# A recommendation tower (CIN and dense layers): three instead of four GpSimd adds per block, a sum of 14 instead of ten parts

## The reference

```python
e = jnp.stack([tbl_0[ids[:, 0]], ..., tbl_38[ids[:, 38]]], axis=1)      # (512, 39, 16)
def _cin_layer(X0, Xi, W, b):
    Wr = W.reshape(H, F0_, Fi)
    return jnp.einsum('hjk,bjd,bkd->bhd', Wr, X0, Xi) + b[None, :, None]
for W, b in Ws:                       # three layers, X0 = e throughout
    Xi = _cin_layer(X0, Xi, W, b)
    res.append(Xi.sum(axis=2))        # (512, 128) each
h = jnp.concatenate([z, dense_ctx], axis=1)          # z: the three, (512, 384)
h = jnp.maximum(h @ W_top1 + b_top1, 0.0)
h = jnp.maximum(h @ W_top2 + b_top2, 0.0)
y = h @ W_top3
```

## Time and profile before

| | us |
|---|---|
| median of 3 runs | 710.0 (707.98 to 715.27) |
| profiled execution | 709.59 |
| its span, first to last instruction | 707.8 |
| TensorE busy | 650.3 (92%) |
| VectorE busy | 506.6 (72%) |
| GpSimd busy | 490.1 (69%) |
| ScalarE busy | 479.0 (68%) |

### The profile page before, as it was taken

The page is one execution under the profiler, slowest core; times in us unless marked ns, Lnnn a source line. Parts: engine busy times, 40 slices in busy tenths (PEclk is TensorE's granted clock), DMA queues, the critical chain, the costliest instruction groups (busy, mean ns, idle before and its releaser), DMA issues.

```text
span 707.8 us, 12139 instructions
## 1 busy us (share of the span) xinstructions
PE 650.3 (92%) x2622; PEld 469.6 (66%) x2622; DVE 506.6 (72%) x1177; ACT 479.0 (68%) x1730; POOL 490.1 (69%) x465
## 2 busy tenths in 40 slices
PE   0097889999999999999999999999989999999998
PEld 0055567777677777777787677777767777778763
DVE  2345588979697979798853797979777979784810
ACT  2145577878687878686935778787767868784802
POOL 5767478878787878888854787878786845453700
PEclk9999999999999999999999999999999999999999
DMA  8660425151515151515140041322323040002000
GB/s 208 126 131 12 110 38 114 40 109 27 120 29 118 28 119 28 120 28 118 29 109 13 10 113 17 81 49 67 63 61 67 7 116 4 2 4 81 0 1 0
DMA packets 65776, 44.51 MB, mean 63 GB/s; under 512 B 49563, under 2 KB 58062, under 8 KB 63860
## 3 DMA queue, kind: packets, MB, share of 16 engines
q1 hardware_dynamic: 54610, 39.35, 25.1%
q0 software_dynamic: 5120, 1.29, 2.1%
q10 hardware_dynamic: 6002, 3.39, 1.8%
HBM read 40.78 MB, written 1.94 MB: 60 GB/s over the span
## 4 chain that ended last, share of the span: by engine, by line
PE 71%; DVE 8%; DMA 6%; issue 4%; POOL 4%; SPq 3%; ACT 3%; DVEq 0%; ACTq 0%; POOLq 0%
PE a_ps L525 28%; PE d_ps L525 18%; PE quad_ps L495 11%; DVE x2t L436 6%; PE quad_ps L568 5%; PE g_ps L555 5%; POOL emb L214 3%; ACT parts L697 2%; DMA rows<-x_rows 2%; DVE parts L424 2%; DMA x_rows<-emb 2%; DMA emb<-tables_dram,rows_now 1%; SPq L320 1%; PE a_ps L654 1%; POOL parts L227 1%
## 5 line engine op out<-in xcount | busy, mean ns | idle before, releaser
L697 ACT ACTIVATE parts<-a_ps,xt 128x128 f32<-128x128 f32 x1536 | 426.5, 397 | 117.9 <-PE a_ps L525 113.6
L227 POOL TENSOR_TENSOR parts<-parts 128x512 f32<-128x512 f32 x256 | 327.3, 1294 | 143.8 <-ACT parts L697 141.4
L424 DVE SCALAR_TENSOR_TENSOR parts<-d_ps,xt,parts 128x128 f32<-128x128 f32 x832 | 236.0, 343 | 90.0 <-PE d_ps L525 82.4
L525 PE MATMUL a_ps<-w_hi,x_hi 128*128 128x512 f32 x384 | 178.0, 464 | 1.8 <-ACT x_hi L668 0.9
L214 POOL DMA_INDIRECT emb<-tables_dram,rows_now x160 | 154.0, 962 | 29.1 <-issue 20.6
L436 DVE TENSOR_REDUCE x2t<-parts 128x128 f32<-128x1280 f32 x64 | 157.4, 2459 | 4.2 <-POOL parts L227 4.2
L525 PE MATMUL a_ps<-w_hi,x_lo 128*128 128x512 f32 x384 | 153.6, 400 | 2.9 <-DVE z L405 2.5
L525 PE MATMUL a_ps<-w_lo,x_hi 128*128 128x512 f32 x384 | 152.3, 397 | 1.2 <-ACT xt L678 1.2
L495 PE MATMUL quad_ps<-products,w_sb 117*128 117x512 f32 (+1 forms) x224 | 116.6, 606 | 13.0 <-DVE products L395 13.0
L525 PE MATMUL d_ps<-w_hi,x_hi 128*128 128x512 f32 (+1 forms) x256 | 124.3, 486 | 0.0
L525 PE MATMUL d_ps<-w_lo,x_hi 128*128 128x512 f32 (+1 forms) x256 | 97.6, 381 | 2.5 <-DMA diag<-xt 2.5
(11 more groups left out here) (52 smaller groups left out, 278.1 us busy)
## 6 DMA issues: line engine op xcount, KB each, us to landing
shifted<-x_rows SPq DMA_DIRECT2D x48, 312.0 KB
shifted<-x_rows SPq DMA_DIRECT2D x48, 234.0 KB
diag<-xt SPq DMA_DIRECT2D x256, 4.9 KB
rows<-x_rows SPq DMA_DIRECT2D x48, 78.0 KB
emb<-tables_dram,rows_now POOLq DMA_INDIRECT x160, 2.4
g_sb<-w_dram ACTq DMA_DIRECT2D x3, 832.0 KB, 10.4
w_sb<-w_dram SPq DMA_DIRECT2D x7, 320.0 KB, 3.0
x_rows<-emb SPq DMA_DIRECT2D x32, 40.0 KB
```

What stands on the lines that cost most here:

```text
L227: nc.gpsimd.tensor_tensor(parts[:, i % 2, now:now + GF, :], parts[:, i % 2, now:now + GF, :], parts[:, i % 2, more:more + GF, :], ALU.add) ...
L424: nc.vector.scalar_tensor_tensor(now, d_ps[d % D_RING][:, H * at:H * (at + 1)], xt[:, u, i, j:j + 1], before, ALU.mult, ALU.add).then_inc( ...
L525: return nc.tensor.matmul(bank[:, 0:H * len(fields)], x[:, u, 128 * i:128 * (i + 1)], w[:, fields[0]:fields[-1] + 1, :].rearrange("p j h - ...
L697: last = nc.scalar.activation(parts[:, i % 2, 2 + GF * a + at, :], a_ps[(NA * i + a) % A_RING][:, H * at:H * (at + 1)], ACT.Copy, scale=xt ...
```

## The change

One more of ScalarE's groups is kept as it is: `KEEP` becomes 3 and `PARTS_LEFT` 2 + 3 x 4 = 14. GpSimd adds groups three, four and five onto groups zero, one and two, so no add builds on an earlier one, and the wait at L225 falls away. An add has to wait for the staging of one group more than the add with the same index did. Since there are only three adds in a block, the ten gathers get new places in the same order. Their number, the other engines' programs and all tiles stay.

```diff
@@ -48,7 +48,7 @@
 D_RING, A_RING = 2, 3
 
 
-ADDS = 4
+ADDS = 3
 KEEP = NA - ADDS
 PARTS_LEFT = 2 + KEEP * GF
 
@@ -79,7 +79,7 @@
 FIRST_TILES = 4
 
 ROWS_AT, FIRST_ROWS_AT, SECOND_ROWS_AT = {(1, 4): 2}, {(1, 0): 1, (3, 4): 2}, {(2, 2): 2}
-GATHER_AT = {(0, 1): 0, (0, 3): 1, (1, 1): 2, (1, 2): 3, (1, 3): 4, (2, 1): 5, (2, 3): 6, (3, 1): 7, (3, 2): 8, (3, 3): 9}
+GATHER_AT = {(0, 1): 0, (0, 2): 1, (1, 0): 2, (1, 1): 3, (1, 2): 4, (2, 0): 5, (2, 1): 6, (2, 2): 7, (3, 1): 8, (3, 2): 9}
 
 W2_STEP = FIELDS // HALF_CHUNKS + 1
 W2_FIRST = FIELDS - W2_STEP * (HALF_CHUNKS - 1)
```

## The result

The changed kernel takes 743.67 us in the median of four runs (740.66 to 747.12) against 710.75 us; the ratio is 1.045 (95% interval 1.040 to 1.050). Its profiled execution took 742.4 us, with a span of 740.6. The forecast was 739, between 722 and 746.

The account below looks back on a forecast made before the run. It took TensorE to bound the kernel, held up by VectorE's sum in VectorE's own queue. Terms 30.4 + 2.2 - 0.3 - 2.8 = +29.5 us on 709.6 gave 739.1, stated as 739, range 722 to 746.

Parts of the forecast that it names:

- item 1: Third-block sums of chunks 1 to 14, chunk 14's fourth, three in chunk 15: 18 delays of 0.95 us reach TensorE.
- item 2: Fourth-block sums without slack, chunks 0 to 13 except 11: 13 times, each passing on 0.95 us.
- item 3: Chunk 0, VectorE's product behind the second block's sum, for which TensorE waits 1.58 us: another 0.95 us.
- item 7: First block: sum longer by 0.95 us, but one GpSimd add fewer to wait for, -1.29: net -0.3 us.
- item 5: VectorE's idle gaps before the next third-block sum absorb too little: 0.18 us left in 12 chunk-to-chunk steps, 2.2 us.
- gathers: Last gather of a chunk issued 1.4 us earlier, shortening TensorE's weight-load waits for ScalarE: -2.8 us, ends 0 and -6.3.
- The sum's price: VectorE's sum (L436) reading 1792 instead of 1280 elements: +0.95 us each, between +0.54 and +1.00.
- proportional: Reading of the sum's price with no fixed part, its whole time scaling with elements: +0.98 us.
- 137-ns reading: Reading of the sum's price with 137 ns fixed, from contiguous products: 1.81 ns per element, +0.93 us.
- Item 4: First- and second-block sums: 1.12 us of slack hides the added 0.95 us, with 0.17 left.
- cheap-element rival: VectorE's sum: further elements cost 1.06 ns each, +0.54 us per sum, total 723 us; chance 11%.
- VectorE's idle time: Rival: 5.9 us idle per chunk swallows the 3.8 us added, total 706.5 us, within 1%; chance 6%.

Follow-up runs that it names:

- changed kernel's second run: The changed kernel, unaltered, measured again: median 741.8 us against 712.5 for the kernel before; its profiled execution took 735.4 us.
- six-part sum: Sum of third and fourth blocks after five adds (three in first and second), against the kernel before: 720.9 us; with gathers ahead of adds 704.0 us.
- GpSimd's side: Changed kernel with three adds and moved gathers, but VectorE's sum reading only ten parts: 707.2 us, ratio 0.993 to the kernel before.
- dealt-out version: Kernel before with three, three, five, five adds per block: 720.9 us with the last gather behind the fifth add, 704.0 us with gathers ahead.
- long sum alone: Kernel before, four adds and old gathers kept, with every VectorE sum reading 14 parts instead of ten: 749.1 us, ratio 1.052.
- long third and fourth sums: Kernel before, four adds, with only third- and fourth-block sums of each chunk reading 14 parts: 736.8 us, ratio 1.034.
- long first and second sums: Kernel before, four adds, with only first- and second-block sums of each chunk reading 14 parts: 718.2 us, ratio 1.007.

## Why the prediction was right

The direction, the place and the mechanism were those forecast; the size came out right in part by luck, since two errors of opposite sign met: the sum was 3.5 us too large for executions at equal clock, and it had no term for the clock, which added to the medians. The terms of its sum, with what the trace of the changed kernel's second run, at clock 0.995, has from one `g_block` to the next, against the trace of before:

| term | forecast | measured |
|---|---|---|
| item 1, 18 sums | 17.1 | 15.1 (0.84 each) |
| item 2, the 12 sums in chunks 1 to 13 | 11.4 | 9.5 (0.79 each) |
| first chunk (rest of item 2, items 3 and 7) | 1.6 | 1.8 |
| item 5, remainder | 2.2 | 0.9 |
| chunk 8's first block | not in the sum | 0.6 |
| gathers | -2.8 | -1.9 |
| sum | 29.5 | 26.0 (by the spans 25.8) |

- **The sum's price** was forecast at 0.95 us and is 0.87. Both the proportional and the 137-ns reading overshot. With the six-part sum there are now three sizes in steps of 512 bytes: 1542, 2459 and 3330 ns for 768, 1280 and 1792 elements, so (3330 - 1542) / 1024 = 1.75 ns per element and some 0.2 us fixed. The start-up, taken from contiguous products as 137 ns, was too small; with 0.2 us the same reading gives 0.90. The rest is no more than what the ten-part sum's mean differs by between runs (2444 to 2473 ns). This makes 31 x 0.08 = 2.5 us of the difference.
- **Items 1 and 2** held. TensorE's matmul row books 32 waits (18 + 13 and chunk 8's first block), and the split of the sums (24.4 against 4.7 us) is what slack of 0 and of 1.1 us makes. The weight load's 19th wait, which the prediction did not place, is 0.2 us behind the fourth-block sum of chunk 0, one of item 2's. The slack of the fourth-block sum was about 0.05 us (0.84 less 0.79), nil but for that.
- **The first chunk** is no test of its terms. The wait of item 3 grew as forecast, from 1.58 to 2.43 us, but the chunk's stretch of half clock lay at 63.5 us in the kernel before and at 92.2 in this execution, and in the changed kernel's first profiled execution the chunk took 5.6 us longer, not 1.8. That 1.6 and 1.8 agree is luck.
- **Item 4** held in the steady chunks (9.92 and 9.07 us from sum to sum, not longer than before) and was overlooked in the first block of chunk 8, behind layer 2.
- **Item 5**, the remainder at the fourth block, was too large: at 0.87 us there is 0.87 - 0.77 = 0.10 left, and 0.07 a chunk was measured.
- **The gathers**: the waits of weight loads for ScalarE fell from 6.3 to 0.2 us, and this brought 1.7 us in three places of the chunks 3, 7 and 11, where ScalarE's lateness had really reached TensorE. The other 0.2 lies later in chunk 11. Run by itself, GpSimd's side brought 4.8 us (2.3 to 7.3), part of it clock; its trace is 0.2 us ahead at the end of the first chunk and 3.1 at the end.
- **What the forecast left out** is TensorE's clock, below: some 4.5 us of the medians, an estimate. The medians differ by 32.9 and 29.4 us, the executions at equal clock by 25.8.

Of the signs named beforehand, the chunk (forecast 39 us, measured 38.5), GpSimd's busy time (407, 411.5) and the one wait of the sum for its adds were as said. The weight load was to wait some 30 times and waited 45; it is the matmul row that counts 32, and the 14 short waits of the first blocks were not foreseen. ScalarE's wait for the rows was to fall to a few us: it fell to 17.5, since the first chunk's rows are gathered ahead of all adds, and only the later waits went. The sum was to be 3.41 us and is 3.33. The cheap-element rival (3.0 us for the sum) fell with that. VectorE's idle time did swallow something, 1.9 of 3.4 us per chunk: the whole of the first- and second-block sums, and nothing of the others.

## What to carry to other kernels

Before work is moved from an engine that is busy to one that looks free, read for each place where it lands how long its result can come late: here the same 0.87 us cost nothing in two blocks of a steady chunk and nearly its full length in the two others, and dealing the work out by that slack, with the gathers in the right places, beat both kernels. And take what an operation's reads cost from a row with the same steps between elements: the same sum took 2.0 or 3.3 us. When the order of adds and DMA issues in one queue is changed, look at the DMAs too: with the last gathers behind the fifth add the dealt-out version was 1.1% slower than the kernel before, with them ahead of it 1.0% faster.

## What the hardware did that was not expected

TensorE's granted clock falls from its upper level of 2.4 GHz to 1.2 GHz for short stretches within a run, in every kernel, in other places from one execution to the next. In the changed kernel's first profiled execution, by windows (us, busy time of each engine, granted clock):

```profile
421.50:424.00 2.50, 1.51 (x5) 0.92 (x6) 2.50 (x7) 0.89 (x4) 2.34 (x3) 1.00 0.00 0
424.00:427.40 3.40, 3.40 (x9) 2.61 (x9) 3.37 (x10) 1.56 (x6) 1.60 (x2) 0.50 0.05 4
```

Ahead of the fall TensorE had been busy 1.51 of 2.50 us, waiting 1.16 us for `x2t` and 0.42 for `x_lo`. The seven other falls within the profiled executions of the kernel before and of the changed kernel's two came within 1.6 us of the end of a wait of 2.3 to 2.8 us for products, for a DMA or for `z`, waits that both kernels have. Not every such wait was followed by a fall: in the kernel before, none followed the 2.49 us at 91.82. In the run of the long sum alone the same happened near the end, and for longer:

```profile
700.00:706.50 6.50, 5.34 (x20) 3.11 (x18) 6.41 (x13) 4.21 (x16) 5.04 (x4) 1.00 0.00 0
706.50:720.50 14.00, 13.87 (x16) 3.67 (x14) 2.67 (x1) 0.09 (x1) 0.00 (x0) 0.51 0.00 0
```

Here TensorE had been busy 5.34 of 6.50 us. From each execution's span and mean clock the time at half clock is estimated as 2 x (1 - clock) x span. Over 59 executions of the kernel before it was 0 to 30 us, 11.7 in the mean, and by a straight line through them each microsecond of it went with 0.42 us more time. Over the eight of the changed kernel it was 7 to 34 us, 22.5 in the mean: (22.5 - 11.7) x 0.42 = 4.5 us of the changed kernel's loss. That the longer waits bring this about is likely but not shown: with the long sum alone it was 30 us in the mean of four, but with the long third and fourth sums, which wait nearly as much, 14 in the mean of five, and other stretches with the same waits stayed at full clock.

The same 0.42 us sets the partial runs right. Taken off every execution, this estimate leaves the mean of the long sum alone 28.3 us above the kernel before on the same chip, that of the long first and second sums 3.7 us and that of the third and fourth 23.9 us, together 27.6. GpSimd's side alone is at -3.7, and 28.3 - 3.7 = 24.6 us against 25.7 for the changed kernel's second run. So the parts add up to the whole once the clock is taken out, and with it they do so only roughly.
